# Ten pieces of expert weights, issued between row loads instead of ahead of the loop

## The reference

```python
h = tok(x, W, b, pos_embd)                          # patches -> 256
h = concatenate([cls_tok, h], axis=1)               # 32 x 37 tokens
h = h + attn(layernorm(h), Wq, Wk, Wv, Wo, ...)     # causal, 16 heads
h = h + ffn(layernorm(h), ...)
# ffn: router, 6 of 32 experts per token, one shared expert, one of 16 "anchors"
routed = einsum('te,teh->th', cw, silu(x w_gate[e]) * (x w_up[e]) @ w_down[e])
anchor = (the same with the one anchor of the token, hidden size 64)
out = routed + shared + 0.1 * anchor
```

## Time and profile before

| | |
|---|---|
| median of 3 runs | 419.11 us (416.32 to 420.45) |
| profiled execution | 413.89 us |
| its span in the trace | 412.1 us |
| mean granted clock of PE | 0.93 |
| PE busy | 343.3 us, 83% of the span |
| DVE busy | 278.0 us, 67% |
| ACT busy | 190.0 us, 46% |
| POOL busy | 181.7 us, 44% |
| moved by DMA | 88.44 MB, 215 GB/s in the mean |

### The profile page before, as it was taken

How to read it: one execution, slowest core, us unless ns; L and a number is a source line. 1 busy time by engine, 2 the same in 40 slices (tenths; PEclk the granted TensorE clock), 3 DMA queues, 4 the chain that set the end, 5 groups by cost and what they waited for, 6 DMA issues and landing times.

```text
span 412.1 us, 8817 instructions
## 1 busy us (share of the span) xinstructions
PE 343.3 (83%) x2552; PEld 299.1 (73%) x2552; DVE 278.0 (67%) x1171; ACT 190.0 (46%) x471; POOL 181.7 (44%) x159
## 2 busy tenths in 40 slices
PE   5999999999899968773889999999999999994000
PEld 3786978779687857561677789999999999993000
DVE  0466789989798886798357775555565665666675
ACT  1152153441545233400157777777877777771000
POOL 6000000588888768767871374344422344433000
PEclk9999999999999997985989999999999999998555
DMA  7999999986698643694555576555555559531998
GB/s 234 298 335 335 329 341 328 420 320 119 123 337 252 126 96 86 218 387 137 152 162 130 167 214 180 162 158 165 165 145 162 166 155 291 168 113 58 303 303 245
DMA packets 55823, 88.44 MB, mean 215 GB/s; under 512 B 16145, under 2 KB 46521, under 8 KB 55513
## 3 DMA queue, kind: packets, MB, share of 16 engines
q1 hardware_dynamic: 38192, 67.66, 52.9%
q0 software_dynamic: 16720, 19.48, 17.8%
q10 hardware_dynamic: 864, 0.73, 0.6%
HBM read 50.62 MB, written 37.09 MB: 213 GB/s over the span
## 4 chain that ended last, share of the span: by engine, by line
PE 60%; DVE 20%; DMA 8%; issue 3%; ACT 3%; SPq 3%; DVEq 2%; POOLq 0%
PE B L823 20%; PE B L838 10%; PE B L514 6%; PE B L812 5%; DMA W<-sums_d 4%; PE B L549 4%; PE B L632 3%; PE B L598 2%; PE B L618 2%; DVEq L319 2%; DMA e_sb<-rows_d 2%; SPq L419 2%; DVE ring L1589 1%; PE B L656 1%; DMA W<-in_pt 1%
## 5 line engine op out<-in xcount | busy, mean ns | idle before, releaser
L457 POOL DMA_INDIRECT rows_d<-spent,slot x77 | 104.1, 1352 | 97.3 <-issue 90.9
L823 PEld LDWEIGHTS B<-e_sb,UPW 128*128 128x128 f32 x796 | 105.4, 193 | 10.7 <-issue 5.5
L823 PE MATMUL B<-e_sb,UPW 128*128 128x128 f32 x796 | 108.9, 278 | 1.5 <-issue 1.5
L1597 DVE TENSOR_TENSOR e_sb<-e_sb,B 128x128 f32<-128x128 f32 (+1 forms) x112 | 32.3, 288 | 62.2 <-ACT e_sb L990 55.8
L981 ACT COPY UPW<-W 128x512 f32 (+1 forms) x112 | 63.9, 570 | 22.2 <-issue 13.9
L838 PE MATMUL B<-W,e_sb 128*128 x224 | 69.3, 391 | 0.8 <-DVE e_sb L1597 0.8
L483 POOL DMA_INDIRECT sums_d<-spent x32 | 31.1, 972 | 48.7 <-DVE spent L1589 47.9
L812 PE MATMUL B<-ident,e_sb 128*128 128x128 f32 x224 | 43.1, 274 | 1.9 <-DMA e_sb<-rows_d 1.8
L990 ACT ACTIVATE e_sb<-B 128x128 f32<-128x128 f32 (+1 forms) x112 | 30.9, 276 | 22.2 <-PE B L823 20.8
L514 PE MATMUL B<-W 128*111 128x256 f32 (+1 forms) x132 | 34.2, 406 | 4.6 <-DMA W<-in_pt 4.5
L483 POOL DMA_INDIRECT sums_d<-W,tok_full x24 | 23.2, 966 | 30.3 <-ACT W L995 29.7
(11 more groups left out here) (250 smaller groups left out, 524.0 us busy)
## 6 DMA issues: line engine op xcount, KB each, us to landing
e_sb<-rows_d SPq DMA_DIRECT2D x112, 161.0 KB, 2.3
rows_d<-spent SPq DMA_DIRECT2D x2, 7728.0 KB, 44.4
W<-in_wx SPq DMA_DIRECT2D x1, 6643.0 KB
W<-sums_d SPq DMA_DIRECT2D x13, 448.0 KB, 9.4
W<-in_wx SPq DMA_DIRECT2D x10, 516.5 KB, 9.5
W<-in_wx SPq DMA_DIRECT2D x1, 4576.0 KB, 18.7
W<-in_pt SPq DMA_DIRECT2D x4, 666.0 KB, 6.9
W<-sums_d SPq DMA_DIRECT2D x7, 336.0 KB, 11.1
```

The lines of the kernel that those rows point to most:

```text
L457: pool.indirect_dma_start(rows_d, bass.IndirectOffsetOnAxis(ap=slot[0:n, t, j:j + 1], axis=0), xrow[0:n, t, :], None).then_inc(done, 16)
L823: mm = pe.matmul(B[2 + i % 2][:, m * P:(m + 1) * P], UPW[:, i % 2, at:at + P], GT[:, i % 2, k, :], start=k == 0, stop=k == KC - 1)
L1597: dve.tensor_tensor(out[0:n, i % 2, :], S[0:n, i % 2, :], ups, ALU.mult).then_inc(H_ok, 1)
```

## The change

The loop over the ten pieces becomes a function `load_last_weights(p)`, and the loop over the row loads calls it: behind row load 1 comes piece 0, behind row load 2 piece 1, and so on up to piece 9 behind row load 10. The pieces, their sizes, their semaphore and those who wait for it stay as they are. The wait for `h2_ok` now stands ahead of the row loads with the other waits.

```diff
             sp.wait_ge(h2_ok, NT)
-            for p in range(LATE_PIECES):
+
+            def load_last_weights(p):
                 width = -(-(late[2] - late[1]) // LATE_PIECES)
                 lo = late[1] + p * width
                 hi = min(lo + width, late[2])
@@
             for i in range(XT):
                 load_rows(i)
+                if 1 <= i <= LATE_PIECES:
+                    load_last_weights(i - 1)
                 if i == XT - 16:
```

## The result

The changed kernel is slower: 423.69 us against 417.73 us, medians of 18 runs each taken side by side; the ratio is 1.013, with a 95% interval of 1.010 to 1.016, that is 4.3 to 6.6 us. The forecast was 424.7, 5.6 us more than before; between the two medians it is 6.0 us.

A forecast was written before the change was run, and what follows sets the result against it. PE was busy 83% of the span; with pieces, the row loads' queue bounds the loop's start: 205.0 + 9.0 + 5.6 + 5.75 = 225.3, 5.6 us late. 413.89 + 5.6 = 419.5, or 424.7 on the median; range 419.0 to 429.5.

The forecast's parts named there:

- Taking the pieces away gains nothing: Ahead of the loop: SP's 9.43 us of issuing only fill its wait for the table; nothing counted as gain.
- Row 11 decides, 5.6 us late: In the loop: row 11, behind all ten pieces, turned at 225.3 instead of 219.76; bounds 2.9 to 7.7 us late.
- The start: First rows of the loop: piece 0 lands at 205.0; beside scatters a piece costs 1.80 us, a row load 0.575.
- SP itself is late: Rival, chance 0.17: SP's issuing beside slow lookups delays row loads at the loop's start; 7.6 to 10.0 us late.
- The drift: Rows 6 to 11: turns move from 1.29 us apart to about 2, with PE waiting for row loads.
- The prices without scatters: DMA time of all 16 engines once scatters are gone: 1.39 us a piece, 0.63 us a row load.
- Lost time is never regained: Visits after row 11: no spare time, PE busy 8.00 us of 8, so lateness at row 11 stays.
- The scatters last to about 217: POOL's scatters at the loop's start: slowed by pieces beside them, they last to about 217 instead of about 212.
- The pieces' own waiters pay nothing: ACT and PE before the first routed visit: ACT's first weight copy at 239.21, some 14 us behind 225; no cost.
- Hidden: Rival, chance 0.21: six row buffers hide the pieces, as three transfers at 340 us; 0.4 us late, 419.5 on the median.
- Faster: Rival, chance 0.06: no scatter backlog from pieces, so row 1 lands 4.6 us earlier; 414.9 us on the median.
- The estimate from the Trainium skill's figure: Side check on the loop: at 358 GB/s ten pairs take 19.4 us against ten visits of 12.9, 6.5 us late.

The follow-up runs named there:

- e6: The changed kernel with the pieces issued from ACT, one every second visit (0, 2, ... 18): 419.04 against 419.56 us, ratio 1.001.
- e7: The changed kernel with the pieces behind every second row load from the sixth on (6, 8, ... 24), from SP: 419.45 against 419.56 us, ratio 1.001.
- e1: The changed kernel with only 2 of each piece's 1,033 columns behind row loads 1 to 10, the rest loaded ahead of the loop: 419.39 against 417.01 us, ratio 1.008.
- e3: The changed kernel with the whole pieces behind row loads 12 to 21 in place of 1 to 10: 421.25 us, ratio 1.014 to the kernel before.
- e4: The changed kernel with the pieces issued from ACT's queue, one in each of visits 0 to 9: 420.61 us, ratio 1.011 to the kernel before.

## Why the prediction was right, step by step

*Taking the pieces away gains nothing.* Right, and shown by e6 and e7 (1.001, with intervals of some 0.4% to either side). In after the scatters issued from 166 to 180 land in 5.4 us in the median, against 9.1 in before (10.5 from 172 to 179), and the table is no earlier for it: from the end of the attention's last tile (166.34 in before, 168.45 in after) to the table it takes 28.2 and 28.1 us. The scatters' landing, line L460 of after in that stretch:

```profile
DMA to landing us min/median/max: 5.2/5.4/5.7
```

*Row 11 decides, 5.6 us late.* Right in kind, and near in size by luck: counted from the table it is 32.15 - 25.27 = 6.9 us later than in the first profile of before, 7.9 than in the second. But the two parts of this sum were both mis-sized, and made up for each other. **The start** was put too low: with piece 0 landing at 205.0 and three more at 1.80 the sum has row 5 at 205.0 + 3 x 1.80 + 4 x 0.575 = 212.7, 0.5 us late; measured are 4.0 us (21.7 against 17.7). In the profile of after 3.3 of them are there by row 3 (214.34, 17.8 us after the table, against 14.5): rows 2 and 3 left SP in time and landed late, with the DMA engines full; the other 0.7 us are in two visits that PE worked through without a wait. So there it is the term of the sum that was too small, a piece and a row load beside scatters: rows 2 and 3 landed 214.34 - 210.42 = 3.9 us apart, not 1.80 + 0.575 = 2.4. The rival *SP itself is late* came true in that row load 5 went out 210.38 - 196.53 = 13.9 us after the table, where that rival had 209.2 - 194.49 = 14.7; but PE did not wait for it. That SP's issuing by itself can cost is shown by e1, where there are no bytes and rows 3 and 4 are waited for because they went out late. How the loss at the start of the changed kernel divides between the two is not shown, and one profile can't settle it, as row 2 of e3 landed as late with no piece at all. **The drift** was put too high: from row 5 to row 11 the sum adds 5.1 us, measured are 2.9, since a piece and a row load take 1.72 us together and not 1.39 + 0.575 = 1.97 or, beside scatters, 2.4; 0.69 MB in 1.72 us are 404 GB/s. The prices without scatters came from packet times as a share of 16 engines in other stretches. Packet times can overlap (the share above is 1.04), so they can overstate a price; how much of the difference that makes isn't shown. The wait for a row that the pieces make is the mechanism named.

*Lost time is never regained.* Not quite. Behind row 11 the visits of after come 1.1 us apart for a while, not 1.29; by row 16 the 6.9 us have become 5.9, and at row 33 it is still 5.9. The rows that lay waiting let PE and DVE catch up a little.

*The scatters last to about 217.* Right in kind: POOL's second memset starts at 219.71 in after, 23.2 us after the table, where it was 20.0 in before; 3.2 us later, where the prediction had 5.

```profile
219.71 3.26 POOL L483 MEMSET spent<- 128x3791 f32 x1 [5.28 <-issue]
```

*The pieces' own waiters pay nothing.* No wait for them shows in after.

*The rivals.* Hidden: not at this spacing; even with six loads of lead (e3) it cost 1.0 to 1.4%, but with a piece only every second visit it is true (e6, e7). The three transfers that hide at 340 us are 1.2 MB; 5.2 MB at a piece per visit are more than the lead of six row loads takes up. Faster: row 1 was turned some 9.1 us after the table in after and 10.9 in before, which looked like the backlog of that rival; but e7, likewise without pieces ahead, has 9.1, and e4 10.7, and neither is faster.

The estimate from the Trainium skill's figure ("DMA: Bandwidth & Descriptors", Specifications, 358 GB/s), 6.5 us, came near the measured 6.9 by chance: the engines moved about 400 GB/s, more than that figure, ten pairs at the measured 1.72 us are 4.3 us late, and the rest was lost at the start.

Two things stay open. Why SP's issue of a DMA takes up to 2.98 us while scatters run, against 0.43 later, wasn't tried. And the profiles have the change 5.9 to 6.9 us late at row 33, at the upper end of the 4.3 to 6.6 us that the times give; how much of this is the chance of single executions, which moved row 5 by 4.9 us between e3 and e7, can't be told from them.

## What to carry to other kernels

A load that is cheap in an idle stretch isn't free in a loop that streams its own data: add up the DMA time of everything that one iteration moves, by measured bytes per microsecond, and compare it with the iteration; only what fits into it, on the mean over as many iterations as the buffers reach ahead, is hidden. Another queue didn't help against that here; whether it helps against an issuer that is late wasn't tested by itself. So ask the two questions apart: when does the load go out, and when do the engines get to it. At the start of a loop, when every buffer is wanted as it lands, put the loop's own loads out first.

## What was not expected

SP's issue of a small plain DMA (two columns for 128 partitions) took 2.04 us at 210.97 and 0.43 us five microseconds later; scatters took 29% of the 16 engines' time from 210.9 to 213 and 7% from 215.5 to 217.5. Scatters alone don't explain it: the piece at 214.18 took 0.46 us with them at 27%. And the sixteen engines' packet times, which the prices were made of, give 1.97 us for a piece and a row load that came in 1.72.
